# Two layers from parts for four chunks of the last pass of a graph network, with statistics and end steps in other places

## What is computed

```python
def gnn(u, v):                        # 3 rounds; leaky = leaky_relu with slope 0.01
    for _ in range(3):
        v = mlp(adj @ u, uv_W1, uv_b1, uv_W2, uv_b2, uv_W3, uv_b3)
        u = mlp(adj @ v, vu_W1, vu_b1, vu_W2, vu_b2, vu_W3, vu_b3)
    return v
def mlp(x, W1, b1, W2, b2, W3, b3):
    x = leaky(x @ W1 + b1); x = leaky(x @ W2 + b2); return leaky(x @ W3 + b3)
x = layernorm(x + relu(adj @ x @ kernel + bias))
x = layernorm(x + gnn(x, ...))
```

## Time and profile before

| | us |
|---|---|
| median of 3 runs | 1169.57 |
| lowest, highest | 1169.35, 1169.69 |
| the profiled execution | 1169.33 |
| its span, first to last instruction | 1167.5 |
| TensorE busy in the span | 1153.9 (99%) |
| VectorE busy | 737.0 (63%) |
| ScalarE busy | 660.1 (57%) |
| GpSimd busy | 3.3 |

### The profile page before, as it was taken

The page is one execution under the profiler, slowest core; times in us unless marked ns, Lnnn a source line. Parts: engine busy times, 40 slices in busy tenths (PEclk is TensorE's granted clock), DMA queues, the critical chain, the costliest instruction groups (busy, mean ns, idle before and its releaser), DMA issues.

```text
span 1167.5 us, 13724 instructions
## 1 busy us (share of the span) xinstructions
PE 1153.9 (99%) x5242; PEld 953.5 (82%) x5242; DVE 737.0 (63%) x889; ACT 660.1 (57%) x813; POOL 3.3 (0%) x8
## 2 busy tenths in 40 slices
PE   7999999999999999999999999999999999999997
PEld 6888888888888888888888888888888888887876
DVE  7997676458555555555545746553566555678984
ACT  7765555346554555555444754554556544667874
POOL 0000000000000000000000000000000000000001
PEclk9999999999999999999999999999999999999999
DMA  9988775568366646555656736555564656589871
GB/s 383 403 308 321 246 271 193 204 216 288 120 207 215 213 154 212 204 191 180 211 186 216 246 115 220 205 183 184 196 237 166 212 190 225 173 296 359 309 269 36
DMA packets 72353, 261.60 MB, mean 224 GB/s; under 512 B 8032, under 2 KB 8800, under 8 KB 71264
## 3 DMA queue, kind: packets, MB, share of 16 engines
q1 hardware_dynamic: 72144, 260.61, 63.0%
q10 hardware_dynamic: 144, 0.13, 0.0%
HBM read 258.61 MB, written 2.10 MB: 223 GB/s over the span
## 4 chain that ended last, share of the span: by engine, by line
PE 94%; DMA 3%; DVE 2%; ACT 0%; SPq 0%; issue 0%; ACTq 0%
PE agg_ps L923 28%; PE agg_ps L916 28%; PE agg_ps L909 28%; PE pre_ps L820 4%; DMA adj_raw<-in_adj 3%; PE hid_ps L781 1%; PE hid_ps L783 1%; PE hid_ps L782 1%; DVE adj_lo L761 1%; PE hid_ps L842 1%; PE hid_ps L856 0%; ACT adj_hi L628 0%; DVE stats L641 0%; SPq L490 0%; PE hid_ps L859 0%
## 5 line engine op out<-in xcount | busy, mean ns | idle before, releaser
L761 DVE TENSOR_TENSOR adj_lo<-adj_raw,adj_hi 128x1024 fp32r<-128x1024 f32 x464 | 548.1, 1221 | 224.6 <-ACT adj_hi L628 219.2
L909 PE MATMUL agg_ps<-adj_hi,feat_hi 128*128 128x512 f32 x1484 | 586.4, 395 | 7.3 <-ACT adj_hi L628 7.3
L916 PE MATMUL agg_ps<-adj_hi,feat_lo 128*128 128x512 f32 x1484 | 579.2, 390 | 0.0
L628 ACT ACTIVATE adj_hi<-adj_raw 128x1024 fp32r<-128x1024 f32 x464 | 467.6, 1051 | 82.2 <-PE agg_ps L923 69.1
L923 PE MATMUL agg_ps<-adj_lo,feat_hi 128*128 128x512 f32 x1484 | 459.0, 391 | 0.2 <-DVE adj_lo L761 0.2
L909 PEld LDWEIGHTS agg_ps<-adj_hi,feat_hi 128*128 128x128 f32 x1484 | 279.4, 188 | 65.8 <-issue 9.2
L916 PEld LDWEIGHTS agg_ps<-adj_hi,feat_lo 128*128 128x128 f32 x1484 | 279.5, 188 | 59.3 <-issue 1.9
L923 PEld LDWEIGHTS agg_ps<-adj_lo,feat_hi 128*128 128x128 f32 x1484 | 278.8, 188 | 59.9 <-DVE adj_lo L761 1.5
L522 ACT ACTIVATE hid<-hid_ps,params 128x512 f32<-128x512 f32 (+2 forms) x82 | 55.2, 673 | 61.3 <-PE hid_ps L783 50.7
L593 ACT ACTIVATE in_hi<-part 128x512 fp32r<-128x512 f32 x24 | 15.2, 634 | 110.4 <-DVE part L750 110.4
L522 ACT ACTIVATE post<-pre 128x512 f32<-128x512 f32 x39 | 24.7, 633 | 88.0 <-DVE pre L728 88.0
(11 more groups left out here) (80 smaller groups left out, 389.4 us busy)
## 6 DMA issues: line engine op xcount, KB each, us to landing
adj_raw<-in_adj SPq DMA_DIRECT2D x472, 512.0 KB, 5.6
adj_raw<-in_adj SPq DMA_DIRECT2D x8, 1024.0 KB, 8.1
resid<-in_x SPq DMA_DIRECT2D x8, 256.0 KB, 8.0
out<-resid SPq DMA_DIRECT2D x7, 256.0 KB, 5.2
params<-in_weights SPq DMA_DIRECT2D x1, 386.0 KB, 4.9
b_row<-in_bias_rows SPq DMA_DIRECT2D x1, 128.0 KB, 5.4
out<-resid SPq DMA_DIRECT2D x2, 64.0 KB, 1.7
out<-resid ACTq DMA_DIRECT2D x1, 128.0 KB, 2.0
```

Of the source, the lines that this page charges most:

```text
L628: act.activation(split_hi(b)[:, i * CHUNK:(i + pieces) * CHUNK], adj_raw[:, h % RAW, 0:pieces * CHUNK], ACT.Copy).then_inc(adj_hi_ready, 1)
L761: dve.tensor_tensor(split_lo(b)[:, slot], adj_raw[:, h % RAW, 0:pieces * CHUNK], split_hi(b)[:, slot].bitcast(F32), ALU.subtract).then_inc ...
L909: pe.matmul(group_bank(g), feat_hi[feats][:, tile(src, i)], split_hi(b)[:, piece(i)], start=start, stop=False)
L916: pe.matmul(group_bank(g), feat_lo[feats][:, tile(src, i)], split_hi(b)[:, piece(i)], start=False, stop=False)
```

## The change

It does four things. Units 40 to 43 (the new kind `LAST_PARTS`) make both hidden layers from parts, as the middle passes do, with other offsets: `act_in` and `dve_in` are steps of their own now, also for the summed units 42 and 43, and their last steps end 36 pieces behind the closing one instead of 24. The statistics of unit 44 stand one offset later (by a tie they come to piece 1518), those of unit 46 three offsets earlier. The bias matmuls of units 47 to 49 stand later. Unit 47 is normalised by GpSimd behind unit 46, with only the reciprocal on VectorE (`dve_root`), and is stored from ScalarE's queue when GpSimd is done.

```diff
-IN_PARTS, TURN, LATE2, LATE, END, END2 = "in_parts", "turn", "late2", "late", "end", "end2"
+IN_PARTS, TURN, LAST_PARTS, LATE2, LATE, END, END2 = "in_parts", "turn", "last_parts", "late2", "late", "end", "end2"
+LAST_IN_PARTS = 4
 STEPS = {
...
-               act_post=16, dve_stats=16, act_std=20, dve_shift=20, act_norm=24),
+               act_post=16, dve_stats=17, act_std=20, dve_shift=20, act_norm=24),
+    LAST_PARTS: dict(dve_sum=0, act_in=2, dve_in=5, pe_hid1=9, act_hid1=10, dve_hid=13, pe_hid2=17, act_hid2=18,
+                     pe_out=21, dve_pre=22, act_post=25, dve_stats=27, act_std=31, dve_shift=33, act_norm=36),
...
-    END: dict(dve_sum=0, act_in=0, pe_hid1=1, pe_bias=5, act_hid1=3, pe_hid2=5, act_hid2=7, pe_out=9, act_post=10,
-               dve_stats=15, act_std=19, dve_shift=21, act_norm=24),
+    END: dict(dve_sum=0, act_in=0, pe_hid1=1, act_hid1=3, pe_hid2=5, act_hid2=7, pe_bias=7, pe_out=8, act_post=10,
+               dve_stats=15, act_std=19, dve_root=20, pool_norm=20, act_out=24),
...
-            return END2 if after < 0 else END if after == 0 else LATE if after == 1 else LATE2 if after == 2 else LAST
+            return END2 if after < 0 else END if after == 0 else LATE if after == 1 else LATE2 if after == 2 \
+                else LAST_PARTS if u < self.rows * (PASSES - 1) + LAST_IN_PARTS else LAST
...
-        return self.steps_of(u) in (IN_PARTS, TURN)
+        return self.steps_of(u) in (IN_PARTS, TURN, LAST_PARTS)
...
-            first = TILES if plan.on_pool(u) else 0
+            first = TILES if plan.steps_of(u) == LATE else 0
...
-                    sp.wait_ge(pool_normed, 1)
+                    sp.wait_ge(pool_normed, normed_on_pool(u))
...
-                    if plan.steps_of(u) == END:
-                        act.wait_ge(act_normed, normed_by(u, False))
-                        act.dma_start(out[chunk_of(u)][:, own(u)], resid[:, columns_of(u)]).then_inc(out_written, 16)
+                u = at(t, "act_out", (LAST,))
+                if u is not None:
+                    act.wait_ge(pool_normed, normed_on_pool(u))
+                    act.dma_start(out[chunk_of(u)][:, own(u)], resid[:, columns_of(u)]).then_inc(out_written, 16)
...
-                    dve.reciprocal(moments(u)[1], std[:, :]).then_inc(rstd_ready, 1)
+                    wait_for_normed(dve, plan.first_of(u) - 1)
+                    dve.reciprocal(moments(u)[1][:, tiles], std[:, tiles]).then_inc(rstd_ready, 1)
...
-                u = at(t, "dve_hid", HIDDEN)
+                u = at(t, "dve_hid", DEEP)
...
-                u = at(t, "dve_in", HIDDEN)
+                u = at(t, "dve_in", DEEP)
```

7 lines of the change are left out of this document (5 added, 2 removed).

## The result

| | before | after |
|---|---|---|
| median of the runs, us | 1169.46 (6 runs, 1169.26 to 1169.69) | 1175.13 (6 runs, 1175.07 to 1175.30) |
| ratio to before, with its 95% interval | | 1.0048 (1.0039 to 1.0058) |
| the profiled execution, us | 1169.33, span 1167.5 | 1175.07, span 1173.3 |

The change makes the kernel 5.7 us slower; the forecast was 1174.3. The whole interval lies above 1, so the loss is clear of noise. The lines of the kernel after are seven to ten higher than those of before: the split is L636 (ScalarE) and L771 (VectorE), the sum L760, in_hi L601, in_lo L751, hid_lo L746, the layers from parts L791 to L793, a normalising activation L550. In the kernels of the experiments they move by up to three more, or by one less.

The account below looks back on a forecast made before the run. The prediction took TensorE, 94% of the span, to bound the kernel; -1.5 (layers) - 0.55 (statistics) - 0.7 (end) + 7.7 (waits) = +4.95 on 1169.33 gave 1174.3 us, range 1169.5 to 1177.5.

Parts of the forecast that it names:

- The waits: TensorE idle ahead of layers of units 40, 42 and 43, waiting for low parts from VectorE; +7.7 us in sum.
- eight layers from parts: Two layers in each of units 40 to 43 become cheaper on TensorE than one f32 matmul; -1.5 us.
- first layer of 42: TensorE waits for in_lo behind VectorE's sum and ScalarE's in_hi, splits and normalisation; +2.3 us.
- second layer of 42: TensorE waits for hid_lo behind VectorE's four splits, statistics of unit 41 and shift; +1.2 us.
- first layer of 43: VectorE is 0.7 us late at the sum, then in_lo follows splits and statistics of unit 42; +2.35 us.
- second layer of 43: ScalarE's chain with the normalisation of unit 42 makes hid_lo late for TensorE; +1.45 us.
- gap ahead of unit 45: With unit 44's statistics moved behind unit 45's sum on VectorE, TensorE's largest gap closes; -0.55 us.
- the end: Bias matmuls off the path, a VectorE shift dropped and GpSimd's work and transfers earlier in the tail; -0.7 us.
- P: The start of piece 1456; TensorE reaches unit 42's first layer at P + 5.9, could start at P + 8.2.
- the rival: Clock falls behind TensorE's waits, 2.4 us more for some ten matmuls, 1176.7 us; judged unlikely after 2.3 us; chance 0.05.
- The lock of the ports: VectorE's last steps wait for one GpSimd tile of unit 47, 0.8 us more, 1175.1 us; chance 0.08.
- Free of charge: All waits at units 40 to 43 are covered, so -2.75 us remains, 1166.8 us; chance 0.09.

Follow-up runs that it names:

- unit 42 alone: The changed kernel with only unit 42 made from parts, the other units in the order of LAST; 1175.07 us, ratio 1.0048.
- more room: The changed kernel with the layers of units 42 and 43 at 13 and 23 pieces instead of 9 and 17, second layers of 40 and 41 later; 1172.87 us.
- the later normalisation: The changed kernel with the normalisation of units 40, 41 and 42 set two pieces later; 1174.92 us, ratio 1.0045.
- two units alone: The kernel before with only units 40 and 41 made from parts, their second layer one piece later than in the change; 1169.88 us, ratio 1.0004.
- the kernel without parts: The changed kernel with no unit from parts, keeping the later statistics of units 40 to 44 and the new end; 1169.76 us, ratio 1.0003.
- the parts alone: The kernel before with units 40 to 43 from parts and nothing else of the change; 1175.28 us, ratio 1.0051.
- the end alone: The changed kernel without parts and with statistics at their old places, only the order of LATE, END and END2 new; 1169.33 us, ratio 1.0000.
- 43 alone: The changed kernel with only unit 43 made from parts, the other units in the order of LAST; 1173.08 us, ratio 1.0028.
- work without dependence: The changed kernel with f32 layers at units 42 and 43 that don't wait for the low parts, which are still made; 1171.81 us, ratio 1.0022.

## Why the prediction was right, and where not

| term | predicted | measured |
|---|---|---|
| eight layers from parts | -1.5 | -1.47 |
| second layer of 40 | +0.4 | +0.40 |
| first layer of 42 | +2.3 | +2.20 |
| second layer of 42 | +1.2 | +1.08 |
| first layer of 43 | +2.35 | +2.20 |
| second layer of 43 | +1.45 | 0, and 1.6 for the clock |
| first matmul behind each wait | 0 | 4 x 0.08 |
| gap ahead of unit 45 | -0.55 | -0.65 |
| the end | -0.7 | -0.1 |
| already there at piece 1424 | 0 | +0.16 |
| sum | +4.95 | +5.74, as between the profiled executions |

**The waits: right**, size and mechanism. The sum of unit 42 was put 1.4 us behind P; it starts 1.3 behind (1090.01, P at 1088.70). TensorE was to start at P + 8.2 and starts at P + 8.1. At the first layer of 42 the rows, and those of two other orders (unit 42 alone, more room), show the chain that the steps named, ScalarE's normalisation, then its rounding, then VectorE's subtraction, then the low part; the later normalisation took most of that wait away. For the second layer of 42 and the first of 43 the prediction counted VectorE's own queue, and the rows show that. What the steps didn't see, because each wait was counted in one order, is how little it helps to move one of them: in three experiments (the later normalisation, more room, two units alone) a wait that was taken away came up again at a later layer. Where their expectations failed, it was in the same way: a step's new place was taken as free, where it stood behind or ahead of other work.

**The second layer of 43: wrong.** The step that failed is the rival's sentence that 2.3 us should not bring the clock down, drawn from the end of the kernel before, where the clock falls 4.7 us behind the start of the last matmul. That was one reading: in the kernel after it falls 3.6 us behind its last matmul (1167.65), and with units 40 and 41 alone 1.8 behind (1162.49; the granted clock is 0.64 in 1164 to 1165). And behind the waits it fell when TensorE was at work again. And the rival had the price wrong in the other direction too: it put 2.4 us beside the waits, while the slow matmuls covered the wait that was to come next. 1.6 of clock for 1.45 of wait changes the sum by 0.15. That the total came out well here is luck: two errors of nearly the same size took each other's place.

**The moved statistics: right** for what was counted, and incomplete. The row shows why unit 45's sum was late, and unit 44's statistics alone close it. But the same number in the table moves the statistics of units 40 to 43. In the kernel without parts this costs more than it gains (0.49 + 0.25 + 0.18 against 0.64). In the kernel with parts it moves nothing but unit 44, which the norm of 43 pushes anyway: as the parts alone show, the gap at unit 45 would be closed without the moved number too, so the 0.65 came for another reason than the one forecast.

**The end: wrong in size**, and this is most of the 0.8 us by which the forecast was low. The bias products moved as described, 0.44 off the way. But there they had covered something: with them gone, TensorE stands at L852 when ScalarE has just made its input (1164.22, L852 at 1164.27), and at L866 when VectorE has just made unit 48's sum (1164.74, L866 at 1164.88). By the chain of waits L852 takes 0.56 us for its pair instead of 0.43, and L866 0.37 instead of 0.22, so 0.28 comes back; 0.17 is left at the last matmul, in the kernel after as in the kernel with the end alone. The work that hid a short wait was moved away, and the step didn't ask what it had hidden. That this is the reason is read from the rows; no run puts one bias product back. On VectorE the last chain is 3.87 us long instead of 3.92: one small shift is gone, the last two norms take 0.38 and 0.42 instead of 0.34 and 0.35 beside GpSimd. The transfers were to give up to 0.25 and gave nothing: the store from ScalarE's queue now hangs on GpSimd's two tiles (1170.70) as the last one hangs on VectorE (1170.77), and from the issue at 1170.73 to the end of the span it is 2.5 us instead of 2.4.

**The lock of the ports**: no wait of 0.8 us; VectorE's last norms run beside GpSimd's 1.61 us with at most 0.07 more each, as just read, and the add of two SBUF tensors (L719, 1166.90) again takes 0.50 in the middle of GpSimd's 3.13. The Trainium skill ("SBUF — State Buffer", Who interferes with whom) has the shared pair as an exclusive lock and says that an add with two SBUF inputs contends with a GpSimd instruction that reads SBUF; for the add this trace doesn't bear it out, as far as its GpSimd rows, whose spans are rough, can tell.

**Free of charge**, the first rival, was the right forecast for units 40 and 41, but for the 0.4 us at unit 40, and the wrong one for 42 and 43. What tells them apart, as I read it, is that 42 and 43 take a sum: VectorE's sum, ScalarE's in_hi, VectorE's in_lo are two hand-overs more, across two engines that are both served in written order. This is argued, not shown: the units also differ in what stands around them, and no run separates the two.

## What to carry to other kernels

Where two engines in strict order hand work to each other, price a new step by the dependence it adds, by what stands ahead of it on each engine, and by whatever must come behind it (here a norm 12 pieces later pushed units that the change never named); slack in busy time, 12 us of 82 here (6 of it made by the waits themselves), says little about it. Before a wait is repaired by moving one step, follow the two layers behind it, and before a short product is taken off the path at the end, ask which wait it was covering. Try the cheap form first where its input needs no extra hand-over, and keep the steps of the next unit at their old places: that was the one version with parts here in which TensorE waited for nothing.

## What the runs showed of the hardware that I had not expected

The granted clock fell behind single waits, but not in a way that the length of the wait decides. In the profiled executions it fell after 2.3 us (43 alone, 0.2 us behind its end), after 3.8 us (42 alone, 1.1 us behind) and after the second of two waits of 2.2 us (kernel after, 1.2 us behind; the parts alone, 0.5 behind), and after one of 2.7 (the later normalisation, 1.0 behind); it did not after the first of the two, nor after 2.64 and 2.67 us (more room for 42 and 43), nor after 2.1 us (work without dependence). Even one kernel differs between its executions: with 43 alone five had spans of 1170.2 to 1171.9 us and mean clocks of 0.997 to 0.999, and one 1169.6 at 1.000; with more room, three had about 1171.0 and two 1172.4. The step of 1.4 us fits one fall of 1.6, but only the profiled execution of each kernel has a trace, so this is argued and not shown. Each fall seen lasted 3.4 us and cost 1.6. The Trainium skill ("TensorE: Matmul & The Clock Gate", HAM oscillation) describes idle gaps after which the clock falls again and again; these traces agree that a gap can do it, and show it once each, not again and again. What of a gap decides stays open.
